# Reordering the head of a fused attention and FFN kernel: q and k ahead of v, and the first loads of v on GpSimd's queue

## The chip, the cores and the metric

The kernel runs on one core of a Trainium2 chip. The metric is the device time of one execution in microseconds, as the median of the runs; lower is better. The profile is of one execution of its own.

## The reference, cut to what matters

A layer of two blocks on x of shape (4, 1024, 256), in float32. Only the first part of the first block is touched by the change.

```python
def binlinear(x, W, b):                      # sign weights, one scale for each output
    alpha = mean(abs(W), axis=1, keepdims=True)
    return einsum('btc,oc->bto', x, alpha * sign(W)) + b

def attn(x):                                 # 16 heads of 16
    q, k, v = (split_heads(binlinear(x, W, b)) for W, b in ((Wq, bq), (Wk, bk), (Wv, bv)))
    att = softmax(einsum('bhtd,bhsd->bhts', q, k) * 16 ** -0.5)
    return binlinear(merge(einsum('bhts,bhsd->bhtd', att, v)), Wp, bp)

x = x + layernorm(attn(layernorm(x)))
x = x + layernorm(ffn(layernorm(x)))         # ternary weights, hidden 1024, silu and gelu
```

## The kernel before, in words

The program has three blocks with a barrier of all engines at the end of each: `project` (here called the head), `attention` and `tail_ffn`. Each engine has its own list of instructions, written out by hand, and waits on semaphores.

The head treats the first of four batches, 1024 tokens in two blocks u of 512. It normalises x, turns it on TensorE (`turn_x`), and splits it into a high part (`high_of_x`, ScalarE) and a low part (`low_of_x`, VectorE), so that two fast matmuls give the precision of one slow one. `project_qk(u, half)` multiplies both parts with the signs of the weights for two of the four slots of q and k; ScalarE scales and adds the bias (`copy_qk`). The results are split once more, into `part[0]` (high) and `part[1]` (low, `low_of_qk`, VectorE). SP stores these to a scratch in HBM (`store`) and loads them back in the layout that the scores need (`load_rows`, through `load_row`, L199 in the profile). ScalarE issues some of the loads for k.

For v, `mean_weights` forms the means of |W| as a row on TensorE (a float32 matmul), VectorE copies it (`alpha_row`), `project_v(u)` makes v in PSUM, VectorE scales it (`scale_v`, L514), GpSimd adds the bias (`bias_v`, L580), and `load_first_v(u)` (L435) copies the first four heads to where attention reads them. GpSimd also squares q and k (`squares`, L575). `sum_squares` (L728) sums the squares by head, and from their maximum follows a bound (`top`, `product`, `bound`) and the row `shift` (VectorE, L560), which SP writes into the q rows (L477) at the very end. A flag `wide_range` says whether the bound suffices; attention reads it in its first instructions on TensorE, VectorE and SP.

Attention then begins: scores (L1153), exponentials on ScalarE (L1308), and products with v (L1167), which for the first turn wait on `v_loaded`. Its first SP instruction is L957.

The end of the `project` block is recorded under L321: a drain on each engine's queue and an event semaphore.

Of the kernel before, what the change touches and what calls it, by code (L numbers as in the profile page):

```python
# [14 lines left out]
P = 128  # L15
# [6 lines left out]
TILES = BLK // P  # L22
CT = DIM // P
# [289 lines left out]
def project(nc, x, attn_w, attn_wT, attn_b, attn_b_rows, ffn_s, ffn_s3, const, qk_scr, v_scr, m_scr, quads,  # L313
# [7 lines left out]
    with ExitStack() as ctx:  # L321
# [76 lines left out]
        bound_spread = sem("bound_spread")  # L398
        shift_done = sem("shift_done")
        hi_stored = sem("hi_stored")  # L400
        lo_stored = sem("lo_stored")
        lo_first_stored = sem("lo_first_stored")
        v_stored = first.v_stored
# [23 lines left out]
        @block.sync  # L427
        def _(sp):
            def store(s, u, c, done):
                sp.dma_start(qk_rows[s, 0, c, :, :, u * BLK:(u + 1) * BLK],  # L430
                             part[s][u][:, 2 * c:2 * c + 2, :].bitcast(F32)).then_inc(done, 16)

            def load_first_v(u):
                sp.wait_ge(aug_done, u + 1)
                sp.dma_start(quads.v[0][:, TILES * u:TILES * (u + 1), :],  # L435
                             v_aug[u][:, 0, :, :, :].rearrange("p t j n -> p t (j n)")).then_inc(first.v_loaded, 16)

            for u in range(BATCH_BLOCKS):
                sp.dma_start(x_in[u][:, :, :], x_blk[u]).then_inc(x_loaded[u], 16)
                if u == 0:  # L440
                    sp.dma_start(w_tr[:, 0:2, :, :], attn_wT[:, 0:2]).then_inc(tr_loaded, 16)
            sp.dma_start(w_tr[:, 2:4, :, :], attn_wT[:, 2:4]).then_inc(tr_v_loaded, 16)
            sp.dma_start(w_nat[:, :, :], attn_w).then_inc(nat_loaded, 16)
            sp.dma_start(bias[:, :], attn_b).then_inc(small_loaded, 16)
            for i in range(2):
                sp.dma_start(const.bias_row[:, i, :], attn_b_rows[i].partition_broadcast(P)).then_inc(small_loaded, 16)
            sp.dma_start(const.out_row[:, :], ffn_s3.partition_broadcast(P)).then_inc(small_loaded, 16)
            sp.dma_start(const.scales[:, :], ffn_s).then_inc(small_loaded, 16)
            sp.wait_ge(set_done, ALL_SET)
            sp.dma_start(m_scr[1], zeros[:, :].bitcast(F32)).then_inc(v_stored, 16)  # L450

            sp.wait_ge(rows_set, ROWS_SET)
            sp.wait_ge(rows_by_pool, ROWS_SET)
            sp.wait_ge(high_by_dve, 1)
            store(HI, 0, 0, hi_stored)
            sp.wait_ge(low_done, 1)
            store(LO, 0, 0, lo_first_stored)
            sp.wait_ge(hi_stored, 16)
            load_rows(sp, 0, HI, 0)
            sp.wait_ge(high_by_act, 1)  # L460
            store(HI, 1, 0, hi_stored)
            load_rows(sp, 1, HI, 0)
            sp.wait_ge(low_done, 2)
            store(LO, 1, 0, lo_stored)
            sp.wait_ge(lo_first_stored, 16)
            load_rows(sp, 0, LO, 0)
            load_rows(sp, 1, LO, 0)
            load_first_v(0)
            sp.wait_ge(hi_stored, 16 * BATCH_BLOCKS)
            load_rows(sp, 0, HI, 1)  # L470
            sp.wait_ge(lo_stored, 16)
            load_rows(sp, 0, LO, 1)
            load_first_v(1)
            sp.wait_ge(shift_done, 1)
            for hh in range(2):
                at = hh * HALF + STACK
                sp.dma_start(quads.q[0][at:at + 1, :, :].bitcast(F32),  # L477
                             shift[hh * PAIRS:(hh + 1) * PAIRS, :].bitcast(F32)).then_inc(quads.m_loaded[0], 16)

        @block.vector  # L480
        def _(dve):
# [50 lines left out]
            dve.tensor_scalar(alpha[:, :], abs_sum[:, :], 1.0 / DIM, None, ALU.mult).then_inc(alpha_done, 1)  # L532
            low_of_x(0)
            normalise(1)
            dve.wait_ge(alpha_summed, 1)
            dve.tensor_copy(const.alpha_row[:, :, :], alpha_ps).then_inc(alpha_done, 1)
            low_of_x(1)
            dve.wait_ge(qk_copied, 2)
            dve.tensor_copy(part[0][0][:, 0:2, :], qk[0][:, 0:2, :]).then_inc(high_by_dve, 1)
            dve.wait_ge(high_by_dve, 1)  # L540
            low_of_qk(0, 0)
            dve.wait_ge(alpha_done, 3)
            scale_v(0)
            dve.wait_ge(high_by_act, 1)
            low_of_qk(1, 0)
            scale_v(1)
            top_norm(0)
            top_norm(1)
            dve.wait_ge(norms_read, BATCH_BLOCKS)
# [6 lines left out]
                              ALU.mult).then_inc(top_done, 1)  # L556
            dve.wait_ge(top_done, 3)
            dve.tensor_scalar(const.wide_range[:, 0:1], product[:, :], NORMS_LIMIT, None, ALU.is_gt)
            dve.wait_ge(bound_spread, 1)
            dve.tensor_scalar(shift[:, :], zeros[0:HEADS, :].bitcast(F32), bound_ps, HEADROOM / SCALE, ALU.subtract,  # L560
                              ALU.add).then_inc(shift_done, 1)
# [5 lines left out]
        def _(pool):  # L567
# [10 lines left out]
            def bias_v(u):  # L578
                pool.wait_ge(v_scaled, u + 1)
                pool.tensor_tensor(v_aug[u][:, :, :, :, 0:HEAD_DIM], v_aug[u][:, :, :, :, 0:HEAD_DIM],  # L580
                                   v_shaped(const.bias_row), ALU.add).then_inc(aug_done, 1)

            pool.memset(ident[:, :], 0.0).then_inc(filled, 1)
            pool.wait_ge(filled, 1)
# [27 lines left out]
            pool.wait_ge(small_loaded, SMALL)  # L612
            for u in range(BATCH_BLOCKS):
                bias_v(u)

        @block.scalar
        def _(act):
# [31 lines left out]
            act.activation(abs_tr[:, :, :, :], w_tr[:, 2:4, :, :], ACT.Abs).then_inc(abs_done, 1)  # L649
            act.activation(signs[:, 2, :, :], w_tr[:, 2, :, :], ACT.Sign).then_inc(signs_done, 1)  # L650
            act.activation(const.signs_p[:, :, :], w_tr[:, 3, :, :], ACT.Sign)
            high_of_x(0)
            act.wait_ge(rstd_done, 1)
            std_of(1)
            act.wait_ge(alpha_done, 2)
            act.wait_ge(small_loaded, SMALL)
            copy_qk(0, 0)
# [7 lines left out]
            high_of_qk(0, 1)  # L665
            act.wait_ge(rows_set, ROWS_SET)
            act.wait_ge(rows_by_pool, ROWS_SET)
            act.wait_ge(hi_stored, 16 * BATCH_BLOCKS)
            load_rows(act, 1, HI, 1)
            act.wait_ge(top_done, 3)  # L670
            act.activation(bound[:, :], product[:, :], ACT.Sqrt).then_inc(root_done, 1)
# [6 lines left out]
        def _(pe):  # L678
# [8 lines left out]
                i.then_inc(xT_done, 1)  # L687

            def project_qk(u, half):
                pe.wait_ge(x_lo_done, u + 1)  # L690
                pe.wait_ge(signs_done, 1)
                for s in (2 * half, 2 * half + 1):
                    if u:
                        pe.wait_ge(qk_copied, s + 1)
                    for c in range(CT):
                        w = signs[:, s % 2, c, half * P:(half + 1) * P]
                        pe.matmul(qk_ps[:, s, :], w, x_hi[u][:, c, :], start=(c == 0), stop=False)
                        i = pe.matmul(qk_ps[:, s, :], w, x_lo[u][:, c, :], start=False, stop=(c == CT - 1))
                    i.then_inc(qk_done, 1)

            def mean_weights():
# [29 lines left out]

            pe.wait_ge(ident_set, 1)
            turn_x(0)
            mean_weights()
            project_qk(0, 0)
            turn_x(1)
            project_qk(0, 1)
            project_v(0)
            project_qk(1, 0)
            project_qk(1, 1)  # L740
            project_v(1)
            pe.wait_ge(filled, 4)
            sum_squares(0)
            sum_squares(1)
            pe.wait_ge(top_done, 1)
            pe.transpose(top_ps, top[:, :], ident[0:2 * HEADS, 0:2 * HEADS]).then_inc(top_turned, 1)
            pe.wait_ge(root_done, 1)
# [1631 lines left out]
```

## Time and profile before

| | before |
|---|---|
| median of 3 runs | 1174.35 us |
| lowest and highest run | 1172.58, 1175.43 us |
| the profiled execution | 1175.2 us |
| its span | 1173.4 us |
| PE busy | 1138.7 us, 97% |
| ACT busy | 922.8 us, 79% |
| DVE busy | 749.2 us, 64% |
| POOL busy | 96.9 us, 8% |
| mean granted TensorE clock | 0.989 of full speed |

PE is TensorE's matmuls, PEld its weight loads, DVE VectorE, ACT ScalarE, POOL GpSimd, SP SyncE; a q behind a name is the queue of that engine, where transfers are issued. Spans of instructions on POOL are rough.

### The profile page before, as it was taken

Reading aid. Unit: us, or ns where it says so; the run is one execution under the profiler, and the core shown is the slowest. Engines: PE = TensorE matmul, PEld = TensorE weight load, DVE = VectorE, ACT = ScalarE, POOL = GpSimd, SP = SyncE. Lnnn points to the kernel's source line nnn. Section 1 sums busy time; section 2 is a strip of 40 time slices with the busy share of each in tenths; the row PEclk is TensorE's granted clock in tenths of the full one; section 3 lists DMA queues with packets and bytes.
Section 4 is the critical chain, followed back from the end, with each engine's and each line's share of the span. In section 5 each row is a group of like instructions: output and inputs, shape, how many; then the busy total and the mean of one; then the engine's idle time right before and its main releaser. Section 6 shows DMA issues by size and latency. Waiting matters only on the chain.

```text
span 1173.4 us, 21113 instructions
## 1 busy us (share of the span) xinstructions
PE 1138.7 (97%) x8241; PEld 776.9 (66%) x8241; DVE 749.2 (64%) x1162; ACT 922.8 (79%) x1218; POOL 96.9 (8%) x140
## 2 busy tenths in 40 slices
PE   6699999999999999998999999999999999999997
PEld 4233333333333322324999999999999999999997
DVE  8354525363345336795876868768778687687666
ACT  6689999999999999996676676667756766677665
POOL 6001000101010100000010000010100000101000
PEclk9799999999999999998999999999999999999999
DMA  5989758996889769944232431433314314333031
GB/s 184 241 216 231 192 102 191 222 209 104 184 164 202 161 110 238 255 147 172 91 109 75 144 128 25 157 129 108 113 70 144 128 39 161 110 109 130 15 127 56
DMA packets 67319, 167.03 MB, mean 142 GB/s; under 512 B 10390, under 2 KB 27414, under 8 KB 61062
## 3 DMA queue, kind: packets, MB, share of 16 engines
q1 hardware_dynamic: 66924, 165.18, 52.3%
q8 instruction: 70, 1.15, 0.4%
q10 hardware_dynamic: 288, 0.39, 0.2%
q14 instruction: 37, 0.30, 0.1%
HBM read 122.21 MB, written 52.43 MB: 149 GB/s over the span
## 4 chain that ended last, share of the span: by engine, by line
PE 53%; DVE 1%; issue 0%; ACT 0%; ACTq 0%
PE ffn_ps L1891 36%; PE ffn_ps L1829 5%; PE ffn_ps L1830 5%; PE ffn_ps L1904 5%; PE side_ps L1796 1%; PE side_ps L1804 1%; DVE ln_stats L2240 0%; DVE o_sb L2251 0%; DVE o_sb L2248 0%; DVE o_sb L2238 0%; ACT op_hi L2006 0%; DVE ln_mean_var L2242 0%; DVE ln_rstd L2246 0%; DVE op_lo L2146 0%; ACTq L1999 0%
## 5 line engine op out<-in xcount | busy, mean ns | idle before, releaser
L1308 ACT ACTIVATE probs<-s_ps 128x1024 f32<-128x1024 f32 x512 | 475.1, 1146 | 29.0 <-PE s_ps L1153 28.4
L1167 PE MATMUL y_ps<-probs,v_st 128*17 128x512 f32 x2048 | 270.7, 601 | 3.8 <-ACT probs L1308 1.7
L1891 PE MATMUL ffn_ps<-op_hi,W 128*128 128x256 f32 x1024 | 240.5, 279 | 0.0
L1891 PE MATMUL ffn_ps<-op_lo,W 128*128 128x256 f32 x1024 | 240.5, 279 | 0.0
L1153 PEld LDWEIGHTS s_ps<-q_st,k_st 50*128 50x128 f32 x1024 | 88.2, 185 | 209.1 <-ACT probs L1308 172.7
L2146 DVE TENSOR_TENSOR op_lo<-feed,op_hi 128x1024 fp32r<-128x1024 f32 x144 | 175.2, 1222 | 66.4 <-ACT op_hi L2006 66.3
L1153 PE MATMUL s_ps<-q_st,k_st 50*128 50x512 f32 x1024 | 207.3, 469 | 7.9 <-DMA q_st<-shift 7.4
L1891 PEld LDWEIGHTS ffn_ps<-op_hi,W 128*128 128x128 f32 x1024 | 193.3, 189 | 0.3
L1891 PEld LDWEIGHTS ffn_ps<-op_lo,W 128*128 128x128 f32 x1024 | 191.7, 187 | 0.3
L2006 ACT ACTIVATE op_hi<-feed 128x1024 fp32r<-128x1024 f32 x144 | 151.4, 1057 | 49.2 <-DVE feed L2164 21.9
L1891 PE MATMUL ffn_ps<-op_hi,sums_of_w 128*128 128x256 f32 x768 | 185.5, 283 | 0.0
L1891 PE MATMUL ffn_ps<-op_lo,sums_of_w 128*128 128x256 f32 x768 | 185.4, 283 | 0.0
L1891 PEld LDWEIGHTS ffn_ps<-op_lo,sums_of_w 128*128 128x128 f32 x768 | 147.1, 192 | 0.0
L1891 PEld LDWEIGHTS ffn_ps<-op_hi,sums_of_w 128*128 128x128 f32 x768 | 147.1, 192 | 0.0
L2035 ACT ACTIVATE feed<-feed,scales 128x256 f32<-128x256 f32 x192 | 87.0, 502 | 29.2 <-DVE feed L2189 15.6
L1829 PE MATMUL ffn_ps<-x_hi,W 128*128 128x512 f32 x256 | 101.6, 397 | 2.8 <-issue 2.8
L1830 PE MATMUL ffn_ps<-x_lo,W 128*128 128x512 f32 x256 | 101.3, 396 | 0.0
L1973 ACT ACTIVATE gate<-ffn_ps,scales 128x512 f32<-128x512 f32 x64 | 43.9, 686 | 67.6 <-PE ffn_ps L1830 67.6
L1167 PEld LDWEIGHTS y_ps<-probs,v_st 128*17 128x17 f32 x2048 | 34.5, 95 | 81.2 <-issue 73.4
L1333 DVE COPY y_sb<-y_ps 128x512 f32<-128x512 f32 x32 | 22.1, 689 | 103.1 <-PE y_ps L1167 103.1
L2139 DVE SCALAR_TENSOR_TENSOR feed<-ffn_ps,scales,gate 128x512 f32<-128x512 f32 x64 | 47.2, 748 | 37.3 <-PE ffn_ps L1830 37.3
L1904 PE MATMUL ffn_ps<-W,op_hi 128*128 128x256 f32 x256 | 62.0, 284 | 0.6 <-DVE op_lo L2146 0.6
(207 smaller groups left out, 1312.3 us busy)
## 6 DMA issues: line engine op xcount, KB each, us to landing
sums_of_w<-sum_scr SPq DMA_DIRECT2D x48, 1024.0 KB, 5.1
k_st<-qk_scr SPq DMA_DIRECT2D x90, 128.0 KB, 6.8
q_st<-qk_scr SPq DMA_DIRECT2D x90, 128.0 KB, 7.3
w_scr<-ffn_w SPq DMA_DIRECT2D x16, 704.0 KB, 8.0
W<-w_scr SPq DMA_DIRECT2D x16, 704.0 KB, 5.5
y_scr<-y_sb SPq DMA_DIRECT2D x32, 256.0 KB, 3.2
qk_scr<-y SPq DMA_DIRECT2D x24, 256.0 KB, 7.1
qk_scr<-sums SPq DMA_DIRECT2D x24, 256.0 KB, 8.6
```

The costliest lines, as they stand in the source:

```text
L1153: i = pe.matmul(s_ps[a % 3][:, hh, :], k_st[u][rows, pp, s * P:(s + 1) * P], q_st[u][rows, pp, tb * BLK:(tb + 1) * BLK], start=True, stop= ...
L1167: i = pe.matmul(y_ps[32 * j:32 * j + VCOLS, :], v_st[g % 2][:, s, VCOLS * j:VCOLS * (j + 1)], probs[(PAIRS * turn + j // 2) % PROBS][:, j ...
L1308: act.activation(probs[a % PROBS][:, :, :], s_ps[a % 3][:, :, :], ACT.Exp, scale=SCALE)\
L1829: pe.matmul(dst, w, x2_hi[:, c, :].bitcast(form), start=(c == 0), stop=False)
L1830: mm = pe.matmul(dst, w, x2_lo[:, c, :].bitcast(form), start=False, stop=(c == CT - 1))
L1891: mm = pe.matmul(dst[:, a * HB:(a + 1) * HB], w, part[slot][:, kt // 2, cols].bitcast(form), start=(fresh and kt == 0 and a == 0 and part ...
L1904: mm = pe.matmul(dst, part[o % RING][:, s // 2, tokens].bitcast(form), w, start=(first and part is op_hi), stop=(last and part is op_lo))
L1973: act.activation(gate[n % 2][:, :], bank[BANK_ORDER[2 * n % 6]][:, :], ACT.Silu, scale=scales[:, S1_AT + n:S1_AT + n + 1]).then_inc(gate_d ...
L2006: act.activation(op_hi[o % RING][:, :, :], operand(o), ACT.Copy).then_inc(op_hi_done, 1)
L2035: g = act.activation(dst[:, cols], src[:, cols], ACT.Gelu, scale=scales[:, at:at + 1])
L2139: dve.scalar_tensor_tensor(dst, bank[BANK_ORDER[(2 * n + 1) % 6]][:, :].rearrange("p (j t) -> p j t", j=2), scales[:, S2_AT + n:S2_AT + n ...
L2146: dve.tensor_tensor(op_lo[o % RING][:, :, :], operand(o), op_hi[o % RING][:, :, :].bitcast(F32), ALU.subtract)\
```

## The change

TensorE: `mean_weights` and both `project_v` move behind all `project_qk`, and `project_v(1)` stands behind the two `sum_squares`. `project_qk` makes the four products with the high part first, then waits for the low part. ScalarE: `std_of(1)` goes ahead of `high_of_x(0)`. VectorE: the first cast of q and k and the low parts of both blocks for the first half go ahead of the copy of the mean row and of `scale_v(0)`; `scale_v(1)` goes behind the flag. SP: the second high store has a semaphore of its own and goes ahead of the first row loads; the loads of v leave SP and are issued by GpSimd behind each `bias_v`.

```diff
@@ sync
-            def load_first_v(u):
-                sp.wait_ge(aug_done, u + 1)
-                sp.dma_start(quads.v[0][:, TILES * u:TILES * (u + 1), :], ...
             store(LO, 0, 0, lo_first_stored)
+            sp.wait_ge(high_by_act, 1)
+            store(HI, 1, 0, hi_second_stored)
             sp.wait_ge(hi_stored, 16)
             load_rows(sp, 0, HI, 0)
-            sp.wait_ge(high_by_act, 1)
-            store(HI, 1, 0, hi_stored)
-            load_rows(sp, 1, HI, 0)
             sp.wait_ge(low_done, 2)
             store(LO, 1, 0, lo_stored)
+            load_rows(sp, 1, HI, 0)
             sp.wait_ge(lo_first_stored, 16)
             load_rows(sp, 0, LO, 0)
             load_rows(sp, 1, LO, 0)
-            load_first_v(0)
-            sp.wait_ge(hi_stored, 16 * BATCH_BLOCKS)
+            sp.wait_ge(hi_second_stored, 16)
             load_rows(sp, 0, HI, 1)
             sp.wait_ge(lo_stored, 16)
             load_rows(sp, 0, LO, 1)
-            load_first_v(1)
@@ vector
+            dve.wait_ge(qk_copied, 2)
+            dve.tensor_copy(part[0][0][:, 0:2, :], qk[0][:, 0:2, :]).then_inc(high_by_dve, 1)
+            low_of_x(1)
+            dve.wait_ge(high_by_dve, 1)
+            low_of_qk(0, 0)
+            dve.wait_ge(high_by_act, 1)
+            low_of_qk(1, 0)
             dve.wait_ge(alpha_summed, 1)
             dve.tensor_copy(const.alpha_row[:, :, :], alpha_ps).then_inc(alpha_done, 1)
-            low_of_x(1)
-            dve.wait_ge(qk_copied, 2)
-            dve.tensor_copy(part[0][0][:, 0:2, :], qk[0][:, 0:2, :]).then_inc(high_by_dve, 1)
-            dve.wait_ge(high_by_dve, 1)
-            low_of_qk(0, 0)
             dve.wait_ge(alpha_done, 3)
             scale_v(0)
-            dve.wait_ge(high_by_act, 1)
-            low_of_qk(1, 0)
-            scale_v(1)
@@
             dve.tensor_scalar(const.wide_range[:, 0:1], product[:, :], NORMS_LIMIT, None, ALU.is_gt)
+            scale_v(1)
             dve.wait_ge(bound_spread, 1)
@@ gpsimd
+            def load_first_v(u):
+                pool.wait_ge(aug_done, u + 1)
+                pool.dma_start(quads.v[0][:, TILES * u:TILES * (u + 1), :], ...
             for u in range(BATCH_BLOCKS):
                 bias_v(u)
+                load_first_v(u)
@@ scalar
-            high_of_x(0)
             act.wait_ge(rstd_done, 1)
             std_of(1)
+            high_of_x(0)
@@
-            act.wait_ge(hi_stored, 16 * BATCH_BLOCKS)
+            act.wait_ge(hi_second_stored, 16)
             load_rows(act, 1, HI, 1)
@@ tensor
             def project_qk(u, half):
-                pe.wait_ge(x_lo_done, u + 1)
+                slots = (2 * half, 2 * half + 1)
+                pe.wait_ge(x_hi_done, u + 1)
                 pe.wait_ge(signs_done, 1)
-                for s in (2 * half, 2 * half + 1):
+                for s in slots:
                     if u:
                         pe.wait_ge(qk_copied, s + 1)
                     for c in range(CT):
-                        w = signs[:, s % 2, c, half * P:(half + 1) * P]
-                        pe.matmul(qk_ps[:, s, :], w, x_hi[u][:, c, :], start=(c == 0), stop=False)
-                        i = pe.matmul(qk_ps[:, s, :], w, x_lo[u][:, c, :], start=False, stop=(c == CT - 1))
+                        pe.matmul(qk_ps[:, s, :], signs[:, s % 2, c, half * P:(half + 1) * P], x_hi[u][:, c, :],
+                                  start=(c == 0), stop=False)
+                pe.wait_ge(x_lo_done, u + 1)
+                for s in slots:
+                    for c in range(CT):
+                        i = pe.matmul(qk_ps[:, s, :], signs[:, s % 2, c, half * P:(half + 1) * P], x_lo[u][:, c, :],
+                                      start=False, stop=(c == CT - 1))
                     i.then_inc(qk_done, 1)
@@
             turn_x(0)
-            mean_weights()
             project_qk(0, 0)
             turn_x(1)
             project_qk(0, 1)
-            project_v(0)
             project_qk(1, 0)
             project_qk(1, 1)
-            project_v(1)
+            mean_weights()
+            project_v(0)
             pe.wait_ge(filled, 4)
             sum_squares(0)
             sum_squares(1)
+            project_v(1)
             pe.wait_ge(top_done, 1)
```

## Rows read from the trace of the kernel before

**Rows 1.** Windows: stretch, length, busy PE, PEld, DVE, ACT, POOL, clock, DMA.

```profile
39.10:541.00 501.90, 496.78 (x3370) 161.07 (x3370) 257.55 (x483) 475.14 (x512) 26.01 (x30) 0.99 0.80 185
```

**Rows 2.** Timeline of SP's queue, head: start, length, engine, line, operation.

```profile
19.99 3.15 SPq L430 DMA_DIRECT2D qk_scr<-part  x2
...
31.09 0.53 SPq L435 DMA_DIRECT2D v_st<-v_aug  x1
31.66 2.95 SPq L199 DMA_DIRECT2D q_st<-qk_scr  x6
34.66 0.68 SPq L435 DMA_DIRECT2D v_st<-v_aug  x1
35.38 1.43 SPq L477 DMA_DIRECT2D q_st<-shift  x2
```

**Rows 3.** Line L321, the block's end: duration in ns min/median/max, first start.

```profile
L321 ACTq DRAIN  x1: 2512/2512/2512, 32.7 to 32.7; - x1
L321 DVEq DRAIN  x1: 1258/1258/1258, 33.7 to 33.7; - x1
L321 SPq DRAIN  x1: 531/531/531, 36.9 to 36.9; - x1
L321 SPq EVENT_SEMAPHORE  x1: 17/17/17, 37.6 to 37.6; - x1
```

**Rows 4.** Timeline of TensorE and ScalarE at the start of attention.

```profile
39.11 1.65 PE L1153 MATMUL s_ps<-q_st,k_st 50*128 50x512 f32 x6 [7.38 <-DMA q_st<-shift]
...
43.57 1.91 PE L1167 MATMUL y_ps<-probs,v_st 128*17 128x512 f32 x8
...
46.30 1.94 ACT L1308 ACTIVATE probs<-s_ps 128x1024 f32<-128x1024 f32 x2 [0.76 <-PE s_ps L1153]
```

**Rows 5.** Timeline of ScalarE and VectorE in the head.

```profile
12.29 0.29 ACT L620 ACTIVATE std<-mean_var,eps 128x4 f32<-128x4 f32 x1
...
13.77 1.39 DVE L497 TENSOR_SCALAR x_norm<-x_in,mean_var,rstd 128x256 f32<-128x256 f32 x4
15.07 0.68 DVE L536 COPY alpha_row<-v_ps 128x512 f32<-128x512 f32 x1
...
19.93 2.80 DVE L508 TENSOR_TENSOR part<-qk,part 128x1024 fp32r<-128x1024 f32 x1
...
26.39 1.22 DVE L514 TENSOR_TENSOR v_aug<-v_ps,alpha_row 128x1024 f32<-128x1024 f32 x1
...
29.57 0.20 DVE L555 TENSOR_SCALAR product<-top_qk 1x1 f32<-1x1 f32 x1
...
31.76 0.75 DVE L560 TENSOR_SCALAR shift<-zeros,xT_ps 16x1024 fp32r<-16x1024 f32 x1 [1.82 <-PE xT_ps L748]
32.44 2.46 DVE L508 TENSOR_TENSOR part<-qk,part 128x1024 fp32r<-128x1024 f32 x2
```

**Rows 6.** Timeline of TensorE in the head.

```profile
11.12 3.12 PE L706 MATMUL v_ps<-abs_tr,mean_w 128*128 128x512 f32 x4
...
15.94 1.03 PE L685 MATMUL xT_ps<-ident,x_norm 128*128 128x128 f32 x8
...
26.28 1.90 PE L728 MATMUL xT_ps<-square,gather 128*32 128x512 bf16 x8
```

**Rows 7.** Windows from the first v matmul, first block-1 q/k matmul, and attention's start.

```profile
18.69:20.57 1.88, 1.88 (x18) 1.88 (x16) 1.85 (x3) 0.82 (x2) 1.09 (x2) 1.00 0.00 0
20.57:24.31 3.74, 3.74 (x19) 3.01 (x18) 3.29 (x2) 2.42 (x3) 1.89 (x2) 1.00 0.54 205
...
39.00:47.30 8.30, 7.69 (x28) 2.56 (x32) 3.16 (x12) 6.60 (x8) 1.59 (x7) 0.50 0.96 334
```

**Rows 8.** GpSimd: timeline of one square, and line L580 (ns min/median/max).

```profile
19.75 1.90 POOL L575 TENSOR_TENSOR square<-qk 128x1024 bf16<-128x1024 f32 x1 [0.79 <-ACT qk L630]
...
L580 POOL TENSOR_TENSOR v_aug<-v_aug,bias_row x2: 2157/2662/3166, 25.3 to 28.5; 128x1024 f32<-128x1024 f32 x2
```

**Rows 9.** Line L435, the loads of v: from issue to landing.

```profile
DMA to landing us min/median/max: 3.9/4.4/4.9
```

More of the change, by code:

```diff
@@ L400, in project @@
         hi_stored = sem("hi_stored")
+        hi_second_stored = sem("hi_second_stored")
         lo_stored = sem("lo_stored")
@@ L431, in store @@
                              part[s][u][:, 2 * c:2 * c + 2, :].bitcast(F32)).then_inc(done, 16)
-            def load_first_v(u):
-                sp.wait_ge(aug_done, u + 1)
-                sp.dma_start(quads.v[0][:, TILES * u:TILES * (u + 1), :],
-                             v_aug[u][:, 0, :, :, :].rearrange("p t j n -> p t (j n)")).then_inc(first.v_loaded, 16)
             for u in range(BATCH_BLOCKS):
@@ L581, in bias_v @@
                                    v_shaped(const.bias_row), ALU.add).then_inc(aug_done, 1)
+            def load_first_v(u):
+                pool.wait_ge(aug_done, u + 1)
+                pool.dma_start(quads.v[0][:, TILES * u:TILES * (u + 1), :],
+                               v_aug[u][:, 0, :, :, :].rearrange("p t j n -> p t (j n)")).then_inc(first.v_loaded, 16)
             pool.memset(ident[:, :], 0.0).then_inc(filled, 1)
```

## The prediction

> **What bounds the kernel now.** I read the windows first. From 39.1 to 541 us ScalarE is busy 475.1 of 501.9 us [rows 1]: attention runs at the pace of its exponentials. The change touches nothing there; it rearranges the head, the 39.1 us before the first scores. So a microsecond won or lost in the head should be a microsecond of the whole, and only one question matters: what starts attention, and when?
>
> The second view is SP's queue, which issues nearly all the head's transfers. From the second half of the first row (low part of block 0, issued at 22.7) SP is never idle for long: the row loads, the two loads of v (0.53 and 0.68 us), then the two loads of shift from 35.38 to 36.81 [rows 2]. Each issue takes about half a microsecond, so SP is a chain of issues here and not one of transfers.
>
> The third view is the end of the block. SP's drain begins at 36.9 and takes 0.53, to 37.4; the last events stand at 37.6. VectorE's drain had ended at 33.7 + 1.26 = 35.0, ScalarE's at 32.7 + 2.5 = 35.2 [rows 3]. So SP alone holds the barrier. The first score matmul begins at 39.11 [rows 4], 1.5 us after the barrier; the profile names the loads of shift as releaser, but these were issued before the barrier, and TensorE has to load the flag and branch behind it. I take it that the start follows the barrier by 1.5 us: 39.11 = 37.6 + 1.5. The head ends when the slowest engine has come to the end of its list.
>
> **The change, worked through.** I build the new head's times from the old durations, engine by engine.
>
> ScalarE takes `std_of(1)` ahead of `high_of_x(0)`. That is 0.29 us [rows 5] in front of the high part of x, so the low part of x comes some 0.25 later. `normalise(1)` took from 13.77 to 15.16 [rows 5] and now ends at 15.4. TensorE waited for nothing but its own q/k matmuls before turning block 1 at 15.94 [rows 6]; without the mean of the weights (3.12 us [rows 6]) those are done by about 15.1, so block 1 is turned from 15.45, for 1.03 [rows 6], to 16.5. Gain there: 0.5 us. The high part of x(1) goes to 17.6, the low part to 18.8.
>
> VectorE now takes the cast of part 0 while it waits, and `low_of_qk(0, 0)` begins at about 18.85. Before, it took 2.80 us from 19.93, and GpSimd's square held from 19.75 for 1.90, to 21.65 [rows 5, 8]. 22.73 - 21.65 = 1.08: the two-input subtraction seems not to have run at all while GpSimd worked, and then to have run at its undisturbed length (two of them take 2.46 [rows 5]). The same happened once more in the head. In the new order GpSimd has finished its first square by about 18.9 and starts the second at 19.9 (its trigger, the copy of slot 3, hardly moves), so this low part ends at 20.1, 2.6 us earlier. That looks like the prize of the change. It isn't on the path for long: SP, fed earlier, has the q and k loads behind it by 33.5 and saves 1.2 us of issue time for v (0.53 + 0.68 [rows 2]), but then it waits for shift.
>
> Shift now stands at the end of a serial chain. From 16.5 TensorE has 24 q/k matmuls; sixteen took 3.74 [rows 7], 0.234 each, so it is done at 22.2. Then, exposed, mean weights 3.1 (25.3 to 25.4), VectorE's copy of the row 0.68 [rows 5] with two hand-overs (26.15), sixteen v matmuls 1.88 [rows 7] (28.05), the squares 1.90 [rows 6] (30.0), and **project_v(1)**, again 1.88 (31.9): the transpose of `top` is queued behind it on TensorE, although `top` itself is ready at 31.1. The transpose and three tiny VectorE instructions of some 0.2 us each, as product's 0.20 [rows 5], add 0.7: 32.6. Now VectorE takes `scale_v(1)`, 1.22 [rows 5]: 33.85; ScalarE's root and TensorE's spread hide under it. `shift` takes 0.75 [rows 5]: 34.6, against 31.76 + 0.75 = 32.5 before. SP would issue the shift loads in 1.43 [rows 2] to 36.05 and drain by 36.6, 0.8 us earlier than 37.4. By SP alone the change gains 0.8.
>
> What is late next is VectorE and GpSimd together. Behind shift VectorE still has the two last low parts, 2.46 alone [rows 5]. They used to run after GpSimd was done (28.5 + 2.16 = 30.7 [rows 8]). Now `bias_v(1)` on GpSimd waits for `scale_v(1)`, so it wants to begin at 33.9, in the same place. It takes 2.16 undisturbed, 3.17 when it met a VectorE subtraction [rows 8]. So the order is shift (to 34.6), bias (34.6 to 36.75), low part (1.1, to 37.85), low part (1.2, to 39.05). If bias gets in before shift, the same four pieces follow each other and the end is the same. The sum: VectorE's end 39.05 against SP's 37.4, barrier 1.65 us later, at 39.25; first scores 40.8 instead of 39.11. Bounds: if nothing is serialised, VectorE ends at 34.6 + 2.46 = 37.05, and the barrier isn't later than before (36.6 by SP, so at best -0.35). If shift alone does not hold GpSimd off, bias runs 33.95 to 36.1 beside it and the end is 38.4, +1.0. I take +1.65: bias(0)'s 3.17 instead of 2.16 is the nearest row, and it shows GpSimd waiting when VectorE was first.
>
> The Trainium skill, "SBUF — State Buffer", Who interferes with whom, gives the rule by which I would choose too: a two-input VectorE instruction contends with a GpSimd one that reads SBUF, and whichever is first blocks the other wholly; the serial behaviour of the subtractions here agrees (1.08 us after 21.65). It also lets tensor_scalar take the shared ports in a two-port mode, which no row here shows; by it the sum is +1.65, without it +1.0.
>
> The loads of v on GpSimd: no row shows a transfer issued there. Bounds: nothing, and SP's dearest issue of one, 0.68 [rows 2]. I take 0.7, and even twice that is covered: GpSimd is done with bias(1) at 36.75 and has 2.3 us before VectorE's end at 39.05. The first load (bias(0) from 29.6 to 31.8) is free by 32.5. Landing took 3.9 to 4.9 us from issue [rows 9], so v is there by 36.75 + 4.9 = 41.7; its first reader stood at 43.57 [rows 4] and moves to 45.2, a cushion of 3.5. The split of the `hi_stored` semaphore costs nothing: the second store leaves at 22.8 and its readers on SP and ScalarE come after 26. ScalarE's tail (root at 32.5, two issues, the last high part, the table for exp) ended at 35.2 [rows 3]; everything in it moves by no more than the chain that releases shift, 33.85 against 31.76, so it ends by 37.3, covered as well; the high part that the last low part waits for is there at 34.7.
>
> The "DVE blocks DMA" box of the same page speaks against this move: a DMA from GpSimd's queue has its descriptors written by GpSimd, which a two-port VectorE instruction locks out. Beside the second load VectorE runs two-input subtractions, which the page does not count among these, so it changes no term of the sum. No trace here can show it.
>
> **Rivals.** (A) As worked out, +1.65 us: chance 0.5. (B) The late low parts and the bias overlap after all, or an earlier piece of my chain is shorter, so that the end is set by SP: -0.8 to 0, 1173.6 to 1174.4; against it stands the 2.80. Chance 0.2. (C) The slower one: GpSimd's drain at the end of the block waits until its own transfer has landed. That ends at 36.75 + 4.9 + 0.2 = 41.85 instead of 37.6: +4.3, 1178.6. It decides from a landing of more than 2.3 us. Against it: SP's drain took only 0.53 with the shift loads just issued [rows 3]. Chance 0.13. (D) TensorE's clock: attention starts at 0.50 of full speed and stays there until 47.3 [rows 7], after long idleness; ScalarE idles 0.76 in that stretch [rows 4]. TensorE now rests from about 33 to 40.8 instead of 28.2 to 39.1. If it starts at the high level, some 1.2 us come back: +0.4 with A, about -1.5 with B. Chance 0.1. (E) The chain is shorter by more than 3.5 us, or a new stall of such a size appears elsewhere: 0.07.
>
> **The numbers.** The profiled execution took 1175.2 = 1173.4 + 1.8 around the span, 0.9 above the median 1174.35. I set the change against the median: 1174.35 + 1.65 = 1176.0. The three runs lie between 1172.58 and 1175.43, so the measurement itself moves by about 1.4. The range reaches from B with D (1172.9) to C (1178.6). A difference of 0.3%, 3.5 us, is about what a measurement of this kernel can tell from none: A, B and D fall inside it, C mostly just outside. Faster 0.04, same 0.83, slower 0.13.
>
> **What would show it.** `low_of_qk(0, 0)` at 1.1 to 1.3 us instead of 2.80, ending near 20; the transpose of `top` after the last v matmul; shift ending near 34.6; a low part of over 2 us beside bias_v(1); VectorE's drain as the last, near 39.1, and the first scores near 40.8. The prediction is wrong if SP's drain is last again, if GpSimd's is, or if the first scores start before 39.

## The result, and the profile after

| | before | changed |
|---|---|---|
| median, 22 runs each | 1175.76 us | 1178.77 us |
| lowest and highest | 1172.58, 1181.74 | 1175.79, 1186.36 |
| ratio to before | | 1.0026, 95% interval 1.0015 to 1.0037 |
| profiled execution, its span | 1175.2, 1173.4 | 1180.76, 1179.0 |
| last events of the head's barrier | 37.6 | 42.0 |
| first scores begin | 39.11 | 43.59 |

The ratio gives 1175.76 x 0.0026 = 3.1 us more, with an interval of 1.8 to 4.4. That is a loss that 22 runs can tell from none, though still under the 0.3% that the prediction called the same. The median lies 0.2 us above the range.

The changed kernel's block end, on line L321 (ns min/median/max, first start); it answers to [rows 3]:

```profile
L321 ACTq DRAIN  x1: 2513/2513/2513, 34.2 to 34.2; - x1
L321 DVEq DRAIN  x1: 2254/2254/2254, 35.2 to 35.2; - x1
L321 SPq DRAIN  x1: 485/485/485, 36.6 to 36.6; - x1
L321 POOLq DRAIN  x1: 2144/2144/2144, 39.7 to 39.7; - x1
L321 SPq EVENT_SEMAPHORE  x1: 17/17/17, 42.0 to 42.0; - x1
```

SP, which held the barrier before, is drained by 37.1, and VectorE by 37.45. GpSimd is drained only at 41.9, 4.5 us later than SP was in [rows 3], and the barrier opens with it. The rows of GpSimd and SP in the changed kernel's timeline:

```profile
30.16 2.20 POOL L574 TENSOR_TENSOR v_aug<-v_aug,bias_row 128x1024 f32<-128x1024 f32 x1 [5.38 <-DVE v_aug L508]
32.66 0.75 POOL L579 DMA_DIRECT2D v_st<-v_aug  x1 [0.31 <-POOL v_aug L574]
34.55 4.88 POOL L574 TENSOR_TENSOR v_aug<-v_aug,bias_row 128x1024 f32<-128x1024 f32 x1 [1.15 <-DVE v_aug L508]
39.74 0.56 POOL L579 DMA_DIRECT2D v_st<-v_aug  x1 [0.31 <-POOL v_aug L574]
...
30.98 3.16 SPq L199 DMA_DIRECT2D q_st<-qk_scr  x6
35.16 1.41 SPq L471 DMA_DIRECT2D q_st<-shift  x2
```

`bias_v(1)` took 4.88 us instead of 2.2, and the drain began with the second load's issue at 39.74 and lasted 2.14. The profile's landing times of that line end the question of what the drain waits for:

```profile
DMA to landing us min/median/max: 2.0/3.6/5.2
```

The first load took 5.2, the second 2.0. 39.74 + 2.0 = 41.74, and the drain ends at 41.88. VectorE's and TensorE's rows in the changed timeline:

```profile
17.07 0.69 DVE L530 CAST part<-qk 128x1024 fp32r<-128x1024 f32 x1 [1.92 <-ACT qk L630]
19.95 1.22 DVE L502 TENSOR_TENSOR part<-qk,part 128x1024 fp32r<-128x1024 f32 x1
...
33.26 1.20 DVE L508 TENSOR_TENSOR v_aug<-v_ps,alpha_row 128x1024 f32<-128x1024 f32 x1
34.39 0.74 DVE L554 TENSOR_SCALAR shift<-zeros,xT_ps 16x1024 fp32r<-16x1024 f32 x1
35.06 2.35 DVE L502 TENSOR_TENSOR part<-qk,part 128x1024 fp32r<-128x1024 f32 x2
...
9.39 1.94 PE L685 MATMUL xT_ps<-ident,x_norm 128*128 128x128 f32 x8 [9.39 <-DVE x_norm L491]
12.45 2.07 PE L697 MATMUL qk_ps<-x_hi,signs 128*128 128x512 f32 x4 [1.11 <-ACT x_hi L624]
14.32 1.91 PE L702 MATMUL qk_ps<-x_lo,signs 128*128 128x512 f32 x4
16.02 1.69 PE L685 MATMUL xT_ps<-ident,x_norm 128*128 128x128 f32 x8
...
23.16 1.88 PE L711 MATMUL v_ps<-abs_tr,mean_w 128*128 128x512 f32 x4
...
43.59 1.65 PE L1158 MATMUL s_ps<-q_st,k_st 50*128 50x512 f32 x6 [9.96 <-DVE y_ps L1550]
```

The first low part is down from 2.80 us [rows 5] to 1.22 and ends at 21.2 instead of 22.7, as intended. Shift ends at 35.1. The last two low parts take 2.35 together: they met nobody, so GpSimd waited for them and not they for GpSimd. And the first q/k matmuls are slow: the first four average 0.47 us apart, (14.32 - 12.45)/4, the next four 0.43, (16.02 - 14.32)/4, where the kernel before had 0.23 from 14.31 on. TensorE had been slow before its rest from 11.33 to 12.45 already: its first eight transposes, from 9.39, took 1.94 us in both kernels, eight later ones 1.03 [rows 6], and the mean of the weights took 3.12 from 11.12 [rows 6] but 1.88 from 23.16. The granted clock reads 1.00 all the while (window of the changed kernel):

```profile
14.00:16.00 2.00, 2.00 (x6) 1.44 (x5) 1.16 (x4) 0.51 (x1) 0.00 (x0) 1.00 0.00 0
```

How much reaches the end? VectorE copies y 32 times in attention. The first, one late and the last of these copies, in the changed kernel's timeline and then in that of before:

```profile
63.70 0.69 DVE L1338 COPY y_sb<-y_ps 128x512 f32<-128x512 f32 x1 [3.84 <-PE y_ps L1172]
...
502.21 0.66 DVE L1338 COPY y_sb<-y_ps 128x512 f32<-128x512 f32 x1
...
547.66 0.69 DVE L1338 COPY y_sb<-y_ps 128x512 f32<-128x512 f32 x1 [1.41 <-PE y_ps L1172]
```

```profile
59.58 0.69 DVE L1333 COPY y_sb<-y_ps 128x512 f32<-128x512 f32 x1 [3.84 <-PE y_ps L1167]
...
498.08 0.66 DVE L1333 COPY y_sb<-y_ps 128x512 f32<-128x512 f32 x1
...
540.55 0.69 DVE L1333 COPY y_sb<-y_ps 128x512 f32<-128x512 f32 x1 [1.42 <-PE y_ps L1167]
```

The distance is 4.12 us at the first copy and 4.13 at 498 us: attention neither gives back nor adds a thing for 440 us. Only the stretch before the first copy gave 0.36 of the 4.48 at the first scores back. Then this execution loses another 3.0, in a stretch where TensorE's granted clock is down (windows of the changed kernel: length, busy PE, PEld, DVE, ACT, POOL, clock, DMA):

```profile
515.00:520.00 5.00, 3.44 (x22) 0.69 (x22) 4.76 (x11) 4.37 (x5) 1.12 (x1) 0.91 0.40 147
520.00:525.00 5.00, 5.00 (x32) 1.50 (x28) 3.97 (x7) 2.83 (x3) 0.00 (x0) 0.75 0.05 15
```

Such spells fall differently in each profiled execution, so the head's effect is read from the copies up to 498 us, and the table below does that.

### The profile page after: what moved, and what is told of

It is laid out like the page before. It is cut to its first block, busy times and chain, and to the rows that moved or that the text cites. A ratio compares the mean times of both kernels' runs of the same rounds, so it can differ in the third digit from the quotient of the medians.

```text
span 1179.0 us, 21113 instructions
## 1 busy us (share of the span) xinstructions
PE 1139.9 (97%) x8241; PEld 777.2 (66%) x8241; DVE 748.2 (63%) x1162; ACT 923.1 (78%) x1218; POOL 100.8 (9%) x142
## 3 DMA queue, kind: packets, MB, share of 16 engines
q8 instruction: 70, 1.15, 0.4%
## 4 chain that ended last, share of the span: by engine, by line
PE 52%; DVE 1%; issue 0%; ACT 0%; ACTq 0%
PE ffn_ps L1896 36%; PE ffn_ps L1834 5%; PE ffn_ps L1835 5%; PE ffn_ps L1909 5%; PE side_ps L1801 1%; PE side_ps L1809 1%; DVE ln_stats L2245 0%; DVE o_sb L2256 0%; DVE o_sb L2253 0%; DVE o_sb L2243 0%; ACT op_hi L2011 0%; DVE ln_mean_var L2247 0%; DVE ln_rstd L2251 0%; DVE op_lo L2151 0%; ACTq L2004 0%
```

## The experiments

Each kernel was profiled once, and timed 11 or 12 times beside the kernel before. "Copy" is the distance of the second copy of y (78.50 us in the trace of before), in the profiled execution.

| kernel | last drain ends on | barrier | first scores | copy | ratio, 95% interval |
|---|---|---|---|---|---|
| before | SP | 37.6 | 39.11 | 0 | |
| changed | GpSimd | 42.0 | 43.59 | +4.10 | 1.0026 (1.0015 to 1.0037) |
| a_v_on_sp | SP | 40.5 | 42.06 | +3.30 | 1.0018 (1.0002 to 1.0033) |
| a_bias_first | GpSimd | 40.5 | 42.05 | +3.28 | 1.0015 (0.9999 to 1.0031) |
| a_gap | GpSimd | 39.9 | 41.48 | +2.93 | 1.0032 (1.0019 to 1.0046) |
| a_mean_back | GpSimd | 40.2 | 41.82 | +3.24 | 1.0035 (1.0017 to 1.0054) |
| a_fixed | SP | 35.8 | 39.37 | -0.33 | 0.9995 (0.9980 to 1.0010) |
| b_pool_loads | GpSimd | 39.0 | 40.58 | +2.37 | 1.0014 (0.9993 to 1.0034) |
| b_cast_pool | GpSimd | 38.7 | 40.22 | +1.68 | 0.9998 (0.9981 to 1.0014) |
| b_cast_sp | SP | 36.5 | 38.28 | +1.15 | 0.9997 (0.9982 to 1.0012) |
| b_cast_act | SP | 35.1 | 37.40 | -1.22 | 0.9995 (0.9982 to 1.0008) |
| b_warm_only | SP | 38.6 | 40.03 | +0.76 | 1.0003 (0.9988 to 1.0018) |
| b_cast_act_warm | SP | 36.1 | 38.55 | -0.83 | 0.9986 (0.9972 to 1.0001) |

The intervals are 2.6 to 4.8 us wide, as wide as the whole effect, so the ratios say little on steps of 1 us: by them a_gap and a_mean_back are no faster than the changed kernel. The traces tell the mechanisms apart, each by one execution. The distance also changes between the first scores and the second copy, by 0.2 to 0.9 us in most kernels and by 2.0 in b_cast_sp, so a step at the barrier isn't the same step at the end.

### The loads of v back on SP, in the changed kernel (a_v_on_sp)

```diff
 @@ gpsimd
                 bias_v(u)
-                load_first_v(u)
 @@ sync
             load_rows(sp, 0, LO, 1)
+            load_first_v(0)          # issued by SP
             sp.wait_ge(shift_done, 1)
             ...
+            load_first_v(1)
```

> The changed kernel with both first loads of v issued by SP: the first ahead of the wait for shift, the second behind the loads of shift. Theory 1 (GpSimd's drain waits until its own transfer has landed, some 1.5 us more than an empty drain): bias(1) still ends near 39.4, then SP issues at 39.5 for 0.55 and drains for 0.5, so the barrier's last events stand near 40.7 instead of 42.0, and GpSimd's drain ends right behind bias(1), near 39.6. Rival (the drain is long whatever was issued): GpSimd's drain still ends near 41.5 and the barrier stays near 41.7. Time: 1.3 us under the changed kernel by theory 1, the same by the rival.

Its block end:

```profile
L321 POOLq DRAIN  x1: 4987/4987/4987, 34.4 to 34.4; - x1
...
L321 SPq DRAIN  x1: 364/364/364, 40.0 to 40.0; - x1
L321 SPq EVENT_SEMAPHORE  x1: 17/17/17, 40.5 to 40.5; - x1
```

Theory 1 holds. bias(1) again took 4.88, to 39.36, but GpSimd's drain ends at 39.4 with it, and the barrier comes at 40.5, 1.5 earlier. SP's drain took 0.36 with the load of v just issued: it ended at 40.4, and the load, issued at 39.39, landed 2.0 us later, at 41.4. GpSimd's drain waits for the landing of its own transfer, SP's doesn't. Of the 1.5 us at the barrier 0.8 is left at the second copy (3.30 against 4.10).

### The predicted order, forced (a_bias_first)

```diff
+            dve.wait_ge(aug_done, BATCH_BLOCKS)
             for u in range(BATCH_BLOCKS):
                 dve.wait_ge(high_by_act, 2 + u)
                 low_of_qk(u, 1)
```

> The changed kernel, VectorE waiting for bias(1) before its last two low parts: the order of the prediction, forced. Theory 1 (port lock, and the order alone costs 2.7 us of bias(1)): bias(1) takes 2.2 to 2.8 instead of 4.88 and ends near 37.2, GpSimd issues at 37.5 and its drain ends near 39.7; the low parts take 1.2 each and end near 39.6; barrier near 39.8 to 40, 2 us before the changed kernel's 42.0. Rival (bias(1) is slow for another reason, such as the transfers in flight): it stays over 4 us and the barrier moves to 42 or later.

GpSimd's rows in its timeline, and its drain:

```profile
34.46 2.60 POOL L575 TENSOR_TENSOR v_aug<-v_aug,bias_row 128x1024 f32<-128x1024 f32 x1 [1.08 <-DVE v_aug L508]
37.37 0.56 POOL L580 DMA_DIRECT2D v_st<-v_aug  x1 [0.31 <-POOL v_aug L575]
```

```profile
L321 POOLq DRAIN  x1: 2976/2976/2976, 37.3 to 37.3; - x1
```

bias(1) is down from 4.88 to 2.60, and the rival with the transfers falls. It still holds 0.4 more than the undisturbed 2.16 [rows 8]: it wanted to begin at 34.46, while shift ran from 34.30 to 35.03. VectorE's low parts ended at 39.45. The landing took 2.8 instead of 2.0 us, so of 2.3 us that bias(1) won the barrier shows 1.5.

### One gap on VectorE (a_gap)

```diff
+            dve.wait_ge(shift_done, 1)
             for u in range(BATCH_BLOCKS):
                 dve.wait_ge(high_by_act, 2 + u)
                 low_of_qk(u, 1)
```

> The changed kernel with one wait added on VectorE: for its own shift to be done before the two last low parts. Theory 2 (GpSimd was kept out because VectorE's shift and low parts stood back to back with no wait between, so no gap let it in): bias(1) gets in between and takes about 2.6 to 2.9 us, to 37.3, and both low parts end near 39.6, like the forced order. Rival (VectorE keeps the ports for itself whenever it has work): bias(1) stays at 4.9 us and ends near 39.5, barrier at 42.0.

GpSimd and VectorE in its timeline:

```profile
34.19 2.61 POOL L575 TENSOR_TENSOR v_aug<-v_aug,bias_row 128x1024 f32<-128x1024 f32 x1 [1.15 <-DVE v_aug L508]
...
34.02 0.74 DVE L554 TENSOR_SCALAR shift<-zeros,xT_ps 16x1024 fp32r<-16x1024 f32 x1
34.80 4.21 DVE L502 TENSOR_TENSOR part<-qk,part 128x1024 fp32r<-128x1024 f32 x2
```

One wait for the instruction just ahead, which leaves a gap of 0.04 us, gives the turn to GpSimd: bias(1) ends at 36.8, and now VectorE's two low parts take 4.21 instead of 2.35. This is the prediction's A, and the first low part waits for GpSimd (36.80 - 34.80 = 2.0), as [rows 5, 8] had shown. In the changed kernel the low part began at 35.06, before shift had ended at 35.13, and no gap was left. A wait does stand between them in its list too (`high_by_act`), but what it waits for had long come, so it held nothing up: by these two runs what counts is a wait that makes a gap. In the kernel before, the 2.80 us low part stood behind just such a wait, for the cast ahead of it (`high_by_dve`).

### The mean of the weights back in its place (a_mean_back)

```diff
             turn_x(0)
+            mean_weights()
             project_qk(0, 0)
 @@ and behind project_qk(1, 1)
-            mean_weights()
 @@ vector: copy of alpha_ps back ahead of the cast
```

> The changed kernel with the mean of the weights back behind the first transposes on TensorE, and VectorE's copy of it back ahead of the cast; all else as changed. Theory 2 (with the mean gone from there TensorE rested 1.1 us and ran its first eight q/k matmuls 0.47 us apart instead of 0.23, so nothing was gained by starting them earlier, and the mean and its hand-overs then stood in the open, 3.4 us): the first q/k matmuls start near 14.2 but 0.23 apart, are done near 16.1 as before, block 1's q/k are done 0.5 to 1 us earlier than the changed kernel's 23.2, and the v matmuls start right behind them near 23 instead of 26.55; shift comes 2 to 3 us earlier, near 32. The barrier moves less, since GpSimd's bias(1), its transfer and its landing follow: 40 to 41. Rival (TensorE's pace there has nothing to do with the mean): the first q/k matmuls are 0.47 apart again and end near 18.

TensorE in its timeline:

```profile
13.77 1.67 PE L697 MATMUL qk_ps<-x_hi,signs 128*128 128x512 f32 x4
15.28 1.09 PE L702 MATMUL qk_ps<-x_lo,signs 128*128 128x512 f32 x4
16.21 1.04 PE L685 MATMUL xT_ps<-ident,x_norm 128*128 128x128 f32 x8
```

The q/k matmuls begin 1.3 us later than in the changed kernel and are done at 16.4 against 16.2: nothing had been gained by starting them first. The mean follows the first transposes without a rest here, and the slow pace ends with it: the last four q/k matmuls stand 0.23 apart again and the transposes take 1.04 instead of 1.69. Shift ended at 31.67 instead of 35.13, 3.5 us earlier. The barrier moved by 1.8 only: bias(1) met VectorE again (31.09 to 35.96) and its transfer took 3.6 us to land.

### One part alone in the kernel before: loads of v on GpSimd (b_pool_loads), and the cast earlier with it (b_cast_pool)

```diff
 @@ b_pool_loads: sync
-            load_first_v(0)
 ...
-            load_first_v(1)
 @@ gpsimd
                 bias_v(u)
+                load_first_v(u)
 @@ b_cast_pool, besides: vector
+            dve.wait_ge(qk_copied, 2)
+            dve.tensor_copy(part[0][0][:, 0:2, :], qk[0][:, 0:2, :]).then_inc(high_by_dve, 1)
             low_of_x(1)
-            dve.wait_ge(qk_copied, 2)
-            dve.tensor_copy(part[0][0][:, 0:2, :], qk[0][:, 0:2, :]).then_inc(high_by_dve, 1)
```

> The kernel before with nothing but the loads of v moved from SP to GpSimd's queue. Theory 1: bias(1) ends at 30.6 as before, GpSimd is drained by about 33 to 36, and SP loses two issues, so the loads of shift begin at about 34.1 instead of 35.38, the barrier stands at about 36.4 instead of 37.6, and the first scores start near 37.9: 1.2 us faster than before. Rival (transfers on GpSimd's queue are slow to land while SP's are queued, and the drain waits for them): GpSimd's drain is last, at over 37.4, and nothing is gained.

> As b_pool_loads, and VectorE's cast of the first high part of q and k goes ahead of the low part of x(1). Theory 1 (the 2.80 us of the first low part was GpSimd's square, started first during the cast): the cast runs at 17.0, the low part of q and k at 19.3 for 1.2 us and ends near 20.5 instead of 22.7; SP's chain of issues begins 2 us earlier, the loads of shift follow the chain or shift itself (32.5), barrier near 35.3 to 36, first scores near 37: 1.7 to 2.3 us faster than before. Rival (SP's chain is held by the landing of stores, not by their start): no earlier than b_pool_loads.

The drains of b_pool_loads, then of b_cast_pool:

```profile
L321 POOLq DRAIN  x1: 6064/6064/6064, 32.8 to 32.8; - x1
...
L321 SPq DRAIN  x1: 519/519/519, 36.2 to 36.2; - x1
```

```profile
L321 POOLq DRAIN  x1: 6710/6710/6710, 31.8 to 31.8; - x1
...
L321 SPq DRAIN  x1: 567/567/567, 34.2 to 34.2; - x1
```

Both expectations failed on GpSimd's drain, and the rival of b_pool_loads won. SP is drained 0.7 and 2.6 us earlier than in the kernel before, as expected (b_pool_loads ran 0.7 late from the start of SP's chain, which hid half of its 1.2). But GpSimd's drain takes 6.1 and 6.7 us. The second loads, issued at 32.80 and 31.80, landed 5.9 and 6.6 us later, while SP's and ScalarE's row loads were in flight; both drains end 0.1 to 0.2 us behind the landing. Of these two, the one issued earlier was the slower to land.

b_cast_pool shows one more thing. GpSimd's bias(1) and VectorE's shift in its timeline:

```profile
29.32 2.18 POOL L573 TENSOR_TENSOR v_aug<-v_aug,bias_row 128x1024 f32<-128x1024 f32 x1
...
30.25 1.80 DVE L553 TENSOR_SCALAR shift<-zeros,xT_ps 16x1024 fp32r<-16x1024 f32 x1 [0.58 <-PE xT_ps L747]
```

Shift took 1.80 instead of 0.75: it ran in the 0.55 after bias(1) had ended at 31.50. So this tensor_scalar too needs what GpSimd holds. By the Trainium skill, "SBUF — State Buffer", Who interferes with whom, tensor_scalar can run in a two-port mode and then contends with GpSimd; these runs agree, here with shift as the one that waits and in a_bias_first with GpSimd waiting for shift.

### The cast alone (b_cast_sp), and v on ScalarE's queue with it (b_cast_act)

```diff
 @@ b_cast_sp: the cast as in b_cast_pool, v on SP as before
 @@ b_cast_act, besides: v from SP to the end of ScalarE's list
             high_of_qk(1, 1)
+            for u in range(BATCH_BLOCKS):
+                load_first_v(u)      # issued by ScalarE
             act.activation(warm[:, :], eps[:, :], ACT.Exp)
```

> The kernel before with one edit: VectorE's cast of the first high part of q and k ahead of the low part of x(1). The loads of v stay on SP. Theory 2 (GpSimd's drain waits for the landing of its own transfer, which is what b_pool_loads and b_cast_pool lost): the low part of q and k ends near 20.2, shift is done near 31 to 32, SP issues without v to 32.7 as in b_cast_pool plus 1.2 for v, the loads of shift end near 35.3, SP drains to 35.8, barrier near 36.0 instead of 37.6, first scores near 37.5, 1.6 us faster than before. Rival (something else, such as VectorE's last low parts, is next at 37): barrier within 0.5 of 37.6.

> As b_cast_sp, with both loads of v on ScalarE's queue, behind its last high part. Theory 2: SP drains near 34.8 to 35 as in b_cast_pool, ScalarE has two more issues of 0.5 us, 34.4 + 1 = 35.4 to 35.6, its drain does not wait for the landing, so the barrier stands near 35.7, first scores near 37.2: 1.9 us faster than before. Rival (any drain waits for its engine's transfers, SP's being a lucky landing): ScalarE's drain ends over 3 us after its last issue, near 38.5.

The end of the block in b_cast_act, and its first scores in the timeline:

```profile
L321 ACTq DRAIN  x1: 1455/1455/1455, 33.4 to 33.4; - x1
...
L321 SPq DRAIN  x1: 484/484/484, 34.4 to 34.4; - x1
L321 SPq EVENT_SEMAPHORE  x1: 17/17/17, 35.1 to 35.1; - x1
```

```profile
37.40 1.65 PE L1153 MATMUL s_ps<-q_st,k_st 50*128 50x512 f32 x6 [6.81 <-DMA q_st<-shift]
```

The head shrinks as theory 2 has it: barrier at 36.5 and 35.1. ScalarE's loads of v took 4.3 to 4.4 us to land, the second until about 37, but its drain ended at 34.86, 1.6 us after its last issue was done: of the three engines that issue transfers here, only GpSimd's drain waits. The first scores, though, now come 1.8 and 2.3 us behind the barrier, not 1.5: they wait for shift's landing, as the row names. In all kernels whose barrier comes at 37.6 or later the distance is 1.4 to 1.6. And in b_cast_sp the gain of 0.8 at the first scores had turned into a loss of 1.15 at the second copy. The next runs ask why.

### TensorE kept busy up to the barrier (b_warm_only, b_cast_act_warm)

These add matmuls whose results nobody reads; nothing is left out.

```diff
             pe.transpose(top_ps, top[:, :], ident[0:2 * HEADS, 0:2 * HEADS]).then_inc(top_turned, 1)
+            pe.wait_ge(qk_copied, QK * BATCH_BLOCKS)
+            for n in range(8):       # 3 in b_cast_act_warm
+                pe.matmul(qk_ps[:, n % QK, :], signs[:, 0, 0, 0:P], x_hi[0][:, 0, :], start=True, stop=True)
             pe.wait_ge(root_done, 1)
             pe.matmul(bound_ps, ones[:, :], bound[:, :], start=True, stop=True).then_inc(bound_spread, 1)
+            pe.wait_ge(qk_copied, QK * BATCH_BLOCKS)
+            for n in range(24):      # 18 in b_cast_act_warm
+                pe.matmul(qk_ps[:, n % QK, :], signs[:, 0, 0, 0:P], x_hi[0][:, 0, :], start=True, stop=True)
```

> The kernel before with 8 matmuls on TensorE between the transpose of top and the bound, and 24 behind the bound, whose results nobody reads; nothing else is changed. Theory 3 (what attention loses at its start is TensorE's spell at a clock of 0.50, up to 47 us and later, which follows on the idle time from 28.2 to 39.1): TensorE stays at a granted clock of 1.00 through 39 to 47, ScalarE's waits of 0.76, 0.45 and 0.29 us between its first exponentials all but go, and the eleventh exponential begins 1.2 to 1.5 us earlier than the 50.93 of before, with the first scores at 39.1 as before. Rival (the spell comes whatever TensorE does there, from the barrier or the load of the flag): clock 0.50 from about 39 again, and the eleventh exponential near 50.9.

> b_cast_act with 3 and 18 such matmuls of no use. Theory 3: first scores near 37.4 as in b_cast_act, clock 1.00 from there on, the eleventh exponential near 48 instead of 50.02 and 50.93: about 3 us faster than before in all, beyond what the 95% interval leaves open. Rival: no better than b_cast_act, -0.9 at the eleventh exponential.

Windows of b_warm_only; the clock is the third number from the end:

```profile
38.00:40.00 2.00, 0.00 (x0) 0.00 (x0) 0.48 (x1) 0.00 (x0) 0.00 (x0) 1.00 0.10 28
40.00:42.00 2.00, 1.32 (x8) 0.83 (x8) 0.00 (x0) 1.43 (x2) 0.36 (x5) 0.83 0.59 188
42.00:48.00 6.00, 5.76 (x22) 1.38 (x24) 3.17 (x12) 5.24 (x7) 1.23 (x2) 0.50 1.08 381
```

Theory 3 fell. So did the rival of b_warm_only, in that the clock held over the barrier, while that of b_cast_act_warm, no better than b_cast_act, came true. The clock stays at 1.00 through the barrier, and attention does begin at full pace; but it drops to 0.50 between 40 and 42, in the middle of the first scores, and in b_warm_only ScalarE waits 0.76 and 0.35 us, where the kernel before had 0.76 and 0.45. The slow spell was put off, not avoided. The eleventh exponential began at 51.46 and 50.41 instead of the expected 49.5 and 48. Counted from the first scores that is 11.4 and 11.9 us, against 11.8 in the kernel before and 12.6 in b_cast_act, so 0.4 and 0.8 us were won. But the first scores came 0.9 and 1.15 us later than without the matmuls: in both runs the two row loads that SP issues behind its last store took 2.10 and 2.23 us instead of 1.33 and 1.31. Why they did is open.

### The changed order with everything mended (a_fixed)

The edits of a_v_on_sp, a_gap and a_mean_back together.

> The changed kernel with what the other runs pointed to: the mean of the weights back in its place, the loads of v on SP (the first ahead of the wait for shift, the second last), and VectorE's wait for its own shift ahead of the last low parts. Theory 2 (the three are all that made the changed order slow; q and k ahead of v is not itself at fault): shift done near 31.7, bias(1) ends near 33.7, the low parts near 36, SP's last issue by 35.4 to 36, barrier 36.4 to 36.8 and first scores near 38, 1 us earlier than before. Rival (the order itself costs, since v's chain comes last on every engine): barrier later than 37.6.

Its barrier, and the shift loads and first scores in its timeline:

```profile
L321 SPq EVENT_SEMAPHORE  x1: 17/17/17, 35.8 to 35.8; - x1
```

```profile
33.20 1.44 SPq L477 DMA_DIRECT2D q_st<-shift  x2
...
39.37 1.65 PE L1160 MATMUL s_ps<-q_st,k_st 50*128 50x512 f32 x6 [9.96 <-DMA q_st<-shift]
```

The barrier comes at 35.8, 1.8 before the kernel before: the order q and k ahead of v is not at fault. bias(1) took 2.62 and the two low parts 4.21, as in a_gap. But the first scores begin at 39.37, 3.6 us behind the barrier. The loads of shift were issued by 34.6 and landed some 4.7 us later; before, from 36.8 to at most 39.1, it was 2.3. By the y copies a_fixed is 0.3 us ahead of before; by the ratio it can't be told from it.

## Why the prediction was wrong

**The sign and the place were right, the size was not.** Forecast were 1.65 us more, with a cause at the block's end on VectorE and GpSimd; measured are 3.1 (1.8 to 4.4) over all runs and 4.5 in the profiled head. VectorE's drain was to be the last; GpSimd's was, which the prediction had named as a sign of its being wrong. Attention carried 4.13 of it unchanged to 498 us. So the premise that a microsecond of the head is one of the whole holds here from the first copy on, but not as a rule for the stretch before it: b_cast_sp was 0.8 ahead at the first scores and 1.15 behind at the second copy.

**The step that failed: GpSimd's end.** The prediction put bias(1) ahead of the low parts, ended it at 36.75 and gave GpSimd 2.3 us to spare. It ended at 39.43, 2.7 later. The mechanism, one waits wholly for the other, was right (a_gap, a_bias_first); who waits was wrong. I read from bias(0)'s 3.17 that the one who comes first goes first, and from 2.80 that GpSimd gets in between two VectorE instructions. The missing condition is a gap between them, which a wait makes: a_gap adds one and gets my order, with bias(1) at 2.61.

**A term that stood in a rival.** Behind bias(1) come 0.31 of hand-over and a drain of 2.14. C was that mechanism, with a chance of 0.13 and for the reason that SP's drain takes 0.53; what SP's drain does says nothing of GpSimd's. Six drains behind a transfer of GpSimd's own lasted 2.1 to 6.7 us. All six (changed, a_gap, a_bias_first, a_mean_back, b_pool_loads, b_cast_pool) ended 0.1 to 0.2 us behind its landing, which came 2.0, 2.5, 2.8, 3.6, 5.9 and 6.6 us after the issue. C's own time for the barrier, 41.85, lies beside the measured 42.0 by luck: bias(1) ended 2.7 later than I had it, 0.3 of hand-over was left out, and the landing was 2.9 shorter than the 4.9 I took.

**The sum of the barrier.** 39.43 + 0.31 + 2.14 = 41.88, against SP's 37.4: +4.5. Without GpSimd's transfer the same kernel would stand at 40.5 (a_v_on_sp), without the lost turn at 40.5 or 39.9 (a_bias_first, a_gap), with neither and the mean in place at 35.8 (a_fixed).

**The chain to shift** was forecast to end at 34.6 and ended at 35.13, and two errors in it nearly cancelled. I had the first q/k matmuls at 0.234 us each; they took 0.43 to 0.47 and block 1 was turned by 17.7 instead of 16.5. The mean of the weights took 1.88 from 23.16 where I had 3.1, a time read while TensorE was slow. That the mean's old place cost nothing was missed altogether: a_mean_back, with it there, has shift 3.5 us earlier. The granted clock reads 1.00 in both traces at that point, so it doesn't tell of the slow pace, 512 columns in 0.43 us or about that of the 1.2 GHz level. In these rows that pace is there from TensorE's first instruction at 9.39. It ends by 14.6 where the mean follows without a rest (before, a_mean_back) and near 17.5 where TensorE rests for 1.1 us.

**Right, as forecast:** the first low part at 1.22 us (forecast 1.1 to 1.3; it ended at 21.2, not 20.1), the transpose of `top` behind the last v matmul, SP's last issue at 36.6 (36.05) and its drain at 37.1, no stall of the first product with v. D was no part of it: the granted clock was 0.50 from before the barrier until 51.5. The second store's own semaphore did nothing that a trace shows.

**The range** ended at C's 1178.6; the median of 1178.77 just misses it. It was also set against a median of 1174.35 of three runs, where 22 give 1175.76: of the 2.8 between forecast and result, 1.4 is that, and 1.4 the size of the effect.

**Open:** why a transfer takes 2.0 us to land in one place and 6.6 in another (more were in flight in the second, but no run held that apart), and what sets the end of the slow spell at attention's start, 47.7 us in the kernel before and 51.3 in b_cast_sp, whose gain goes there (8.6 and 13.1 us behind the first scores). A version that is shown to beat the kernel before was not found: b_cast_act is 1.2 us ahead at the second copy and 2.0 at 498 us, and its interval still holds 1. Not every distance stays as it is, either: b_pool_loads is 1.5 us behind at the first copy, 2.4 at the second and 3.9 from the third on, at 94 us.

## What to carry to other kernels

Ahead of a barrier, an engine's end is not its last instruction: find whether its drain waits for its own transfers, and don't issue the last one from such an engine. When two engines shut each other out, look for gaps between the instructions of the one: here it kept the other out through the whole run of them until a wait made a gap. A piece of work that looks free to move may be what keeps TensorE busy while its pace comes up, and it is exposed where it lands.

## What was unexpected of the hardware

- GpSimd's drain at the block's end lasted until its own transfer had landed (2.1 to 6.7 us); SP's (0.36 to 0.57) and ScalarE's (1.6 us after an issue that landed after 4.3) did not.
- A single wait, a gap of 0.04 us, between VectorE's tensor_scalar and its subtraction moved 2.3 us from one engine to the other: bias(1) 4.88 or 2.61, the two low parts 2.35 or 4.21.
- A tensor_scalar of 16x1024 waited for GpSimd's addition, 1.80 us instead of 0.75.
- With 32 matmuls of no use ahead of the barrier the granted clock held 1.00 until attention had begun and then fell to 0.50 all the same.
- TensorE's first matmuls ran at half pace (512 columns in 0.43 us instead of 0.23) while the granted clock read 1.00.
- A load of 8 KB, the shift, took over 4 us to land in a_fixed and at most 2.3 in the kernel before.
